# Low halves of the expert weights: three experts early on VectorE, five half by half on GpSimd, and six unread products on TensorE

## The reference, cut to what matters

```
x: (4, 512, 128); 16 heads of 64, one key and value head for all; 8 experts, F = 512, the best 2 per token
x = x + attn(layernorm(x))          # attn: layernorm(g1, b1), q, kv, softmax, out @ Wo, layernorm(g2, b2)
h = layernorm(x).reshape(-1, 128)
probs = softmax(h @ gate_w.T); topw, sel = top_k(probs, 2); topw /= sum(topw)
gu   = einsum('th,efh->etf', h, gate_up_w)            # gate_up_w: (8, 1024, 128)
hact = gu[..., F:] * gelu(gu[..., :F])
out  = einsum('eth,te->th', einsum('etf,ehf->eth', hact, down_w), combine)
x = x + out
```

## Time and profile before

| what | value |
|---|---|
| median of 3 runs | 625.6 us (622.03 to 625.81) |
| profiled execution: time | 624.44 us |
| profiled execution: span in the trace | 622.5 us |
| mean granted TensorE clock | 0.979 |
| TensorE busy | 576.1 us, 93% |
| VectorE, ScalarE, GpSimd busy | 427.3, 302.9, 391.5 us |

### The profile page before, as it was taken

The page is one execution under the profiler, slowest core; times in us unless marked ns, Lnnn a source line. Parts: engine busy times, 40 slices in busy tenths (PEclk is TensorE's granted clock), DMA queues, the critical chain, the costliest instruction groups (busy, mean ns, idle before and its releaser), DMA issues. The chain is left out here.

```text
span 622.5 us, 8805 instructions
## 1 busy us (share of the span) xinstructions
PE 576.1 (93%) x2605; PEld 328.8 (53%) x2605; DVE 427.3 (69%) x817; ACT 302.9 (49%) x568; POOL 391.5 (63%) x324
## 2 busy tenths in 40 slices
PE   8899999999999999989999988999998589999980
PEld 6455454454554454445545444454434377888870
DVE  4876658559746978884686889866578868444433
ACT  2345645356446554453655445465538163555530
POOL 5357667567669855788796569859648534454330
PEclk9999999999999999999999999999999799999995
DMA  6111011010110100070000000000007100230005
GB/s 176 69 70 70 35 37 69 1 69 26 46 52 18 71 0 2 4 287 14 2 1 2 1 6 18 14 2 1 9 2 200 40 18 27 70 92 27 26 10 203
DMA packets 23981, 29.29 MB, mean 47 GB/s; under 512 B 4403, under 2 KB 14901, under 8 KB 23936
## 3 DMA queue, kind: packets, MB, share of 16 engines
q1 hardware_dynamic: 21664, 24.50, 12.0%
q0 software_dynamic: 2272, 4.24, 2.0%
HBM read 13.73 MB, written 15.32 MB: 47 GB/s over the span
## 5 line engine op out<-in xcount | busy, mean ns | idle before, releaser
L1095 ACT ACTIVATE prob<-s_ps 128x512 f32<-128x512 f32 x256 | 150.5, 598 | 181.8 <-PE s_ps L1201 179.8
L1019 DVE TENSOR_REDUCE rowmax<-max_ps 128x1 f32<-128x512 f32 x256 | 173.1, 685 | 81.6 <-PE max_ps L1170 79.6
L950 POOL TENSOR_TENSOR fold<-prob 128x1024 f32<-128x1024 f32 x63 | 149.6, 2374 | 94.5 <-ACT prob L1095 94.0
L1215 PE MATMUL pv_ps<-prob,v 128*64 128x512 f32 x512 | 138.4, 620 | 0.0
L1199 PE MATMUL s_ps<-q_hl,khh 128*128 128x512 f32 x256 | 117.8, 460 | 0.6 <-ACT prob L1095 0.6
L1170 PE MATMUL max_ps<-khh,q_hl 128*128 128x512 f32 x256 | 103.1, 408 | 6.6 <-DVE q_hl L1008 3.3
L1201 PE MATMUL s_ps<-q_hm,kly 65*128 65x512 f32 x256 | 101.9, 398 | 0.0
L1199 PEld LDWEIGHTS s_ps<-q_hl,khh 128*128 128x128 f32 x256 | 48.4, 189 | 78.5 <-ACT prob L1095 60.6
L956 POOL TENSOR_TENSOR psums<-fold 128x512 f32<-128x512 f32 x63 | 81.7, 1297 | 4.9
L1170 PEld LDWEIGHTS max_ps<-khh,q_hl 128*128 128x128 f32 x256 | 48.8, 191 | 26.7 <-DVE rowmax L1019 9.7
L1201 PEld LDWEIGHTS s_ps<-q_hm,kly 65*128 65x128 f32 x256 | 48.6, 190 | 8.9 <-issue 3.4
(11 more groups left out here) (225 smaller groups left out, 800.2 us busy)
## 6 DMA issues: line engine op xcount, KB each, us to landing
sorted_rows<-raw_w SPq DMA_DIRECT2D x36, 260.0 KB, 2.6
raw_w<-in_gate_upT SPq DMA_DIRECT2D x8, 512.0 KB, 7.6
wd<-in_downT SPq DMA_DIRECT2D x8, 256.0 KB, 3.8
raw_w<-parts SPq DMA_DIRECT2D x8, 256.0 KB, 4.3
psums<-sorted_rows SPq DMA_DIRECT2D x22, 65.0 KB, 1.8
x<-in_x SPq DMA_DIRECT2D x4, 256.0 KB, 5.7
out<-x SPq DMA_DIRECT2D x4, 256.0 KB, 2.7
xs_first<-sorted_rows SPq DMA_DIRECT2D x15, 65.0 KB, 1.9
```

What stands on the lines that cost most here:

```text
L950: nc.gpsimd.tensor_tensor(fold[:, :, :], prob[:, head % 4, 0:2, :], prob[:, head % 4, 2:4, :], ALU.add).then_inc(prob_folded, 1)
L1019: nc.vector.tensor_reduce(rowmax[:, group % 2, it, i:i + 1], max_ps[:, k % 2, :], AX_X, ALU.max).then_inc(max_done, 1)
L1095: nc.scalar.activation(prob[:, head % 4, jt, :], s_ps[:, k % 2, :], ACT.Exp, scale=SCALE).then_inc(exp_done, 1)
L1215: last = nc.tensor.matmul(pv_ps[DH * hd:DH * hd + DH, :], v[:, b % 2, jt, :], prob[:, head % 4, jt, :], start=(jt == 0), stop=(jt == JT - 1))
```

## The change

VectorE takes experts 0, 1 and 2 (`VECTOR_LOW = 3`), ahead of and between its first steps of the block; it takes none after `hidden(2)`. GpSimd takes experts 3 to 7, ten halves instead of eight, starts them when VectorE has done its three, and waits after each half until that half's own semaphore has counted. ScalarE rounds experts 0 and 1 before `x_high(1)` and one expert earlier in two later places, so that `wh` is there for VectorE. TensorE runs four products of `headsel` with itself before `turn_in(0)` and two behind it, into `ht_ps`; nobody reads them, and `turn_hidden(0)` overwrites them. TensorE's wait ahead of `gate(6)` is for the new counts.

```diff
-            def low_gate_up(eng, e, done, pieces=1):
+            VECTOR_LOW = 3
+
+            def low_gate_up(eng, e, done):
                 eng.wait_ge(wh_ready, e + 1)
-                for n in range(pieces):
-                    cols = slice(e * GU + n * GU // pieces, e * GU + (n + 1) * GU // pieces)
-                    last = eng.tensor_tensor(wl[:, cols], raw_w[:, cols], wh[:, cols].bitcast(F32), ALU.subtract)
-                last.then_inc(done, 1)
+                cols = slice(e * GU, (e + 1) * GU)
+                eng.tensor_tensor(wl[:, cols], raw_w[:, cols], wh[:, cols].bitcast(F32), ALU.subtract).then_inc(done, 1)
+
+            def low_gate_up_pieces(pool, e):
+                pool.wait_ge(wh_ready, e + 1)
+                for n in range(2):
+                    cols = slice(e * GU + n * F, e * GU + (n + 1) * F)
+                    nc.gpsimd.tensor_tensor(wl[:, cols], raw_w[:, cols], wh[:, cols].bitcast(F32),
+                                            ALU.subtract).then_inc(wl_pool, 1)
+                    pool.wait_ge(wl_pool, 2 * (e - VECTOR_LOW) + n + 1)
...
-                for e in range(2, E - 2):
-                    low_gate_up(pool, e, wl_pool, 2)
+                pool.wait_ge(wl_ready, VECTOR_LOW)
+                for e in range(VECTOR_LOW, E):
+                    low_gate_up_pieces(pool, e)
...
+                def keep_busy(times):
+                    for _ in range(times):
+                        nc.tensor.matmul(ht_ps[:, :], headsel[:, 0, :], headsel[:, :, :].rearrange("p k c -> p (k c)"),
+                                         start=True, stop=True)
+                keep_busy(4)
                 turn_in(0)
+                keep_busy(2)
...
                         if k == RAW_TILES:
-                            pe.wait_ge(wl_ready, 4)
-                            pe.wait_ge(wl_pool, E - 4)
+                            pe.wait_ge(wl_ready, VECTOR_LOW)
+                            pe.wait_ge(wl_pool, 2 * (E - VECTOR_LOW))
```

More of the change, by code:

```diff
@@ L1402, in _ @@
                 tail_vector(dve, "RSPLIT", last_unit, 0)
+                low_gate_up(dve, 0, wl_ready)
                 hidden(0)
+                low_gate_up(dve, 1, wl_ready)
                 tail_vector(dve, "NORM", last_unit, 0)
-                low_gate_up(dve, 0, wl_ready)
+                low_gate_up(dve, 2, wl_ready)
                 tail_vector(dve, "NORM", last_unit, 1)
@@ L1408, in _ @@
                 tail_vector(dve, "NORM", last_unit, 2)
-                low_gate_up(dve, 1, wl_ready)
                 tail_vector(dve, "NORM", last_unit, 3)
                 hidden(2)
-                low_gate_up(dve, E - 2, wl_ready)
-                low_gate_up(dve, E - 1, wl_ready)
                 for k in range(OPEN, NT + 3):
@@ L1464, in _ @@
                 nc.scalar.activation(spare[:, :], ones[:, 0:1], ACT.Gelu)
+                high_weights(0)
+                high_weights(1)
                 x_high(1)
                 gelu(0)
-                high_weights(0)
-                high_weights(1)
+                high_weights(2)
                 gelu(1)
                 x_high(2)
-                high_weights(2)
                 high_weights(3)
+                high_weights(4)
                 take_turned(0)
                 gelu(2)
-                for e in range(4, E):
+                for e in range(5, E):
                     high_weights(e)
```

## The result

| | before | after |
|---|---|---|
| median, 13 runs each | 625.17 us | 620.95 us |
| range | 621.97 to 626.98 | 617.56 to 626.99 |
| profiled execution, span | 622.5 us | 619.0 us |
| from the second block's start to the end | 155.78 us | 151.91 us |

The ratio is 0.9933, with a 95% interval of 0.9912 to 0.9955: 2.8 to 5.5 us faster. The range holds the time, and the forecast of 621.5 is 0.6 off. The ratio leaves out the three slowest runs after (626.8 to 627.0, mean clock 0.969); with all 13 of each, the ratio of the means is 0.996 and that of the medians 0.993.

The account below looks back on a forecast made before the run. TensorE, 93% busy, was held by a 5.63 us stall plus 2.66 of slow clock; of 8.3 us some 3.5 would be won: 624.44 - 3.5 = 620.9, plus half of the profiled run's 1.2 below the median: 621.5, range 618.3 to 625.6.

Parts of the forecast that it names:

- The stall and its cause: Ahead of `down(1)`: TensorE's 5.63 us wait, from VectorE's `wl` stuck behind GpSimd's unbroken halves before `weigh(0)`, would go.
- The products and ScalarE: At the block's start: unread products make `turn_in(0)` 0.3 us late; with ScalarE's extra rounding tile 1 comes 1.3 us later.
- The cover: Ahead of `down(3)`: the new wait of about 4.7 us also covers the 0.6 to 0.8 us TensorE loses at the start.
- Start of the halves, their number and `rstd`: GpSimd's queue: halves start at 480.0, ten take 13.5 us to 493.5, `rstd` ends at 494.65, YADD 3.5 us earlier.
- The case of the sooner GpSimd: Rival, chance 0.12: sends not held up by `wl`, halves without gaps from 477.5 to 489.9, time 617.3 us.
- What is late next: Last batch's layer norm: GpSimd's halves delay `rstd`, so YADD and `down(3)`; of 8.3 us some 3.5 are won.
- The size of the new wait: Ahead of `down(3)`: TensorE arrives at about 493.3 and waits about 4.7 us, until about 498.05.
- Here the waits cost 0.7 us and bring nothing.: Between GpSimd's halves: no VectorE instruction with two SBUF tensors falls there before YADD, so the waits only cost 0.7 us.
- The clock: In the new wait: falls after 3.8 to 4.1 us of silence, costing 2.66 us; holding 0.45, falling 0.28.
- The fast one of the three early runs: 622.03 us against 625.60 and 625.81, taken as a sign that 5.6 us of idleness does not always cost the clock.
- The rival of the falling clock: Clock falls in the new wait ahead of `down(3)`, costing 2.66 us once more: 623.6 us, chance 0.28.
- Dear waits: Rival, chance 0.07: GpSimd's waits cost 0.30 us or more each, `down(3)` only 0.8 earlier, 626.3 us; decided from about 0.28.

Follow-up runs that it names:

- second run: The kernel before with a wait after each of GpSimd's eight halves, no steps moved, no unread products; median 622.15 us, ratio 0.9950.
- fourth run: The changed kernel with five experts on VectorE and three on GpSimd; median 618.52 us of 6 runs, ratio 0.9881.
- third run: The changed kernel without the six unread products; median 621.53 us, ratio 0.9957.
- fifth run: The changed kernel once more, unaltered, on another chip; median 621.75 us against 625.91 for the kernel before, ratio 0.9942.
- first run: The changed kernel without GpSimd's wait after each of its ten halves; median 624.02 us against 625.23 for the kernel before, ratio 0.9989.
- sixth run: The changed kernel without the waits between GpSimd's halves, repeated beside the changed kernel on one chip; median 623.63 us, ratio 0.9997.
- gaps and products: The kernel before, in its old order, with waits between GpSimd's halves and the six unread products; median 620.33 us, ratio 0.9935.

## Why the prediction was right, point by point

- *The stall and its cause.* Right. `weigh(0)` at 483.28 (about 483 forecast), `down(1)` at 487.25 - 0.37 = 486.88 (486.8 forecast), no `wl` over 1.22 us. The second run shows the cause on its own: with gaps, and nothing moved, the two `wl` fell from 10.44 to 3.43 us. That `hidden` is not held up had stood on a row beside GpSimd's sends; now three `hidden` beside halves took 0.68 and 0.69 us in the changed kernel.
- *The products and ScalarE.* Right in size: `turn_in(0)` 468.11 - 0.37 = 467.74, 0.34 late (0.3 forecast); `gate(1)` 1.2 us late (1.3 forecast). The cover was wrong: I had the new wait hide this loss, but taking the products away gave 0.21 of the 0.34 us back ahead of `down(3)`, since the loss also delays VectorE's `wl`, the send beside the third one and so the start of the halves. I said that they can't win anything at this place since the clock had not fallen; one trace without them shows that it can fall there.
- *Start of the halves, their number and `rstd`.* Right. Start 479.63 after taking off 0.37 (479.3 to 480.5 forecast, 480.0 taken), 13.56 us for ten (13.5), YADD at 494.40 (494.7), `down(3)` 3.37 us behind it (3.36). The case of the sooner GpSimd is out: three sends that began beside a `wl` of VectorE took 1.95, 1.42 and 1.66 us instead of 0.97, and each ended 0.84 us behind the end of that `wl`. The inference of the Trainium skill ("SBUF — State Buffer", "Who interferes with whom"), that a tensor_tensor does not hold up the writing of descriptors, does not agree with these rows. In the second run the `wl` of that stretch started at 480.67, 0.12 us after a send had begun, and no send was stretched: a send is held when the `wl` was there first.
- *What is late next.* Right, and tested by the fourth run: four halves fewer, YADD and `down(3)` 3.25 us earlier. The shift reached the end, as forecast: from `down(3)` on it took 120.94 us before and 120.86 after.
- *The size of the new wait.* Off: 3.04 us, 4.7 forecast. GpSimd was as late as forecast; TensorE arrived 1.4 us later than my 493.3. Of this 0.66 is the wait ahead of `down(2)`, since `var_eps` had held up `weigh(1)`; for the rest I had taken the turns a little too short. Since `down(3)` hangs on YADD, this cost nothing.
- *"Here the waits cost 0.7 us and bring nothing."* Wrong. I had sorted VectorE's steps by whether they read two tensors from SBUF and found none in the stretch. `var_eps`, a tensor_scalar from SBUF to SBUF with a single tensor, is held up as well: 0.92 us with gaps, 3.86 without. No run changed the form of `var_eps`, so what in it meets GpSimd is argued, not shown. The same section of the Trainium skill names tensor_scalar among the operations that can take the port pair shared with GpSimd, under conditions on its operands, and the trace agrees. It also says that the second instruction waits until the first has finished; in the unbroken run it sat out the rest of one half and three more. The waits lengthened the run of halves by 1.15 us, not 0.7. Without them the ratios can't be told from 1 (0.9989 and 0.9997), though the two traces still show a shorter second block.
- *The clock.* The split into held and fallen was the right question, the numbers behind it were not. I took 3.8 and 4.1 us of silence from two rows; it fell 2.1 us after TensorE's last work in the third run (494.64 to 496.74), 2.4 us in the fifth (492.55 to 494.96), and 3.0 and 2.9 us in the first and sixth, and held through 3.04 us in the changed kernel. The price of 2.66 us was too high for this place: from `down(3)` to the end it was 0.5 us (fifth run against the profile after) and 1.1 us (third run), while four traces with the clock held beyond the block's start (gaps only, gaps and products, both with five experts) lie between 120.4 and 121.4 themselves. One part of this the windows show: behind the wait the clock stayed low for 2.8 us in the fifth run and 5.9 in the third, against 5.3 before. That TensorE waits for VectorE in these turns anyway would explain the rest; it was not tested. The fast one of the three early runs was no sign about this wait either, since what happens in attention alone moves the time by as much (last section). The rival of the falling clock, at 623.6, was therefore too far up, and the two likeliest cases lie closer together than I had them.
- *Dear waits.* Out: 0.07 to 0.08 us from one half to the next in the chain, 0.12 a half by the comparison with the first run, where 0.28 would have decided it.

The time was right for the stated reasons, GpSimd's queue above all. That it was right to 0.6 us is partly luck: runs of this kernel spread over 9 us, its median on another chip was 621.75, and the missed length of the wait and price of the clock happened not to enter. One step of the mechanism failed, the one on the waits between the halves, and by the medians of the sixth run it would have led to a slower kernel had I acted on it; the cover of the products failed by 0.2 us.

## What to carry to other kernels

When one engine is held up by another's unbroken run of instructions, break the run before you move work: the gaps alone gave 5.3 us of the second block here, the change with its longer GpSimd queue 3.9. Each is one trace against the single trace before, in which the clock had fallen; by the ratios of whole runs (0.9950 and 0.9933) the two can't be told apart. When work is moved onto an engine, look at what stands behind it in that queue; the end of the next stall was readable to 0.3 us from the queue order, though its length was off by 1.7. And weigh who does shared work by engine time: VectorE does an expert in 1.22 us, and in 1.5 to 2.4 beside halves with gaps, GpSimd in 2.7. Two experts more in VectorE's idle stretches gave the fastest kernels here.

## What the runs showed that I had not expected

- An instruction of VectorE with 4 elements a row takes 3.86 us when it starts beside an unbroken run of GpSimd instructions, and 0.17 with none beside it.
- The clock is not a function of the program. At about 270 us TensorE waits 2.1 to 2.6 us for VectorE in every execution, 2.10 in the one after and 2.13 in the one before; the clock fell behind it in one and not in the other:

```profile
270.00:275.00 5.00, 4.95 (x14) 2.48 (x14) 3.88 (x7) 2.27 (x4) 4.52 (x4) 0.66 1.02 386
```

```profile
270.00:275.00 5.00, 4.76 (x19) 2.68 (x21) 4.51 (x8) 2.74 (x5) 4.52 (x4) 1.00 1.02 382
```

Both are windows of the same 5 us: the first fence is the changed kernel, the second the one before. Such falls in attention move the block's start, by up to 7.4 us between the ten executions: it lay at 464.57 and 464.76 us in the two without a fall ahead of the block, and at 472.01 in the one with the most time at the lower level, about 20 us. Where one kernel has two traces, the starts differ by 2.5 and 2.8 us and the rest of the span by 0.4 and 1.4. Why the clock falls in one execution and not in the next stays open; no run here tested it.
